# Even and odd weight rows, a subtraction moved to GpSimd, and three shifted steps in a mixture-of-experts kernel

## What is computed

```python
h = einsum('bsi,bio->bso', x, W[id]) + b[id][:, None, :]          # conditioning, 256 x 256 weights
xf = h.reshape(1024, 256)
y = (silu(xf @ sw1) * (xf @ sw3)) @ sw2                            # shared expert, 352 wide
scores = softmax(xf @ gate_w)                                      # 8 experts
weights, indices = top_k(scores, 2)
for e in range(8):                                                 # experts, 176 wide
    y += cw[:, e:e+1] * ((silu(xf @ rw1[e]) * (xf @ rw3[e])) @ rw2[e])
out = x + y
```

## Time and profile before

| | |
|---|---|
| median of three runs | 119.95 us |
| profiled execution, whole | 120.04 us |
| its span | 118.4 us |
| TensorE matmuls busy | 106.3 us, 90% of the span |
| DVE busy | 67.8 us, 57% |
| ACT busy | 52.2 us, 44% |
| Pool busy | 46.1 us, 39% |
| mean granted TensorE clock | 0.971 of full speed |
| bytes moved by DMA | 19.08 MB, mean 161 GB/s |

### The profile page before, as it was taken

How to read it: one execution, slowest core, us unless ns; L and a number is a source line. 1 busy time by engine, 2 the same in 40 slices (tenths; PEclk the granted TensorE clock), 3 DMA queues, 4 the chain that set the end, 5 groups by cost and what they waited for, 6 DMA issues and landing times.

```text
span 118.4 us, 2226 instructions
## 1 busy us (share of the span) xinstructions
PE 106.3 (90%) x624; PEld 90.0 (76%) x624; DVE 67.8 (57%) x221; ACT 52.2 (44%) x131; POOL 46.1 (39%) x62
## 2 busy tenths in 40 slices
PE   6887997706999999899999999999999999999791
PEld 4676886404678888667799989999999997888570
DVE  1044575037984199867878676577655543024951
ACT  4035575117161693255657755346555655103000
POOL 4360077730776200001653443443453635704400
PEclk9999999965699999999999999999999999999999
DMA  3899999998886257131223343241012110029843
GB/s 72 237 298 276 345 352 371 383 324 226 216 194 235 89 158 201 41 96 48 91 95 106 100 130 119 86 136 59 29 44 83 50 67 21 0 55 383 329 184 118
DMA packets 16737, 19.08 MB, mean 161 GB/s; under 512 B 2338, under 2 KB 13718, under 8 KB 16726
## 3 DMA queue, kind: packets, MB, share of 16 engines
q1 hardware_dynamic: 13302, 12.62, 35.5%
q0 software_dynamic: 1984, 4.46, 10.7%
q10 hardware_dynamic: 1440, 1.86, 4.7%
HBM read 12.64 MB, written 7.21 MB: 168 GB/s over the span
## 4 chain that ended last, share of the span: by engine, by line
PE 73%; DMA 8%; issue 6%; another core or an unknown queue 3%; POOL 3%; DVE 2%; ACTq 1%; ACT 1%; POOLq 1%; DVEq 0%
PE bank L846 52%; DMA y_area<-_out_by_choice_and_token 6%; PE bank L858 6%; PE bank L978 4%; PE bank L1013 4%; DMA _out_by_choice_and_token<-y_area,dest 2%; PE bank L876 2%; PE bank L873 1%; ACTq L306 1%; POOL _out_by_choice_and_token L406 1%; PE bank L875 1%; POOLq L287 1%; POOL cond_area L288 1%; POOL ids_bc L365 1%
## 5 line engine op out<-in xcount | busy, mean ns | idle before, releaser
L406 POOL DMA_INDIRECT _out_by_choice_and_token<-y_area,dest x23 | 23.6, 1025 | 40.7 <-DVE y_area L767 26.4
L394 POOL DMA_INDIRECT rows_by_expert<-h_area,slot x16 | 15.5, 971 | 15.9 <-DVE slot L628 11.6
L846 PE MATMUL bank<-w_all,hsT_hi 128*128 x72 | 21.6, 342 | 0.0
L846 PE MATMUL bank<-hT_area,sh_area 128*128 128x512 f32 (+1 forms) x72 | 18.7, 421 | 0.0
L846 PEld LDWEIGHTS bank<-hT_area,sh_area 128*128 128x128 f32 (+1 forms) x72 | 13.7, 193 | 4.2
L846 PEld LDWEIGHTS bank<-w_all,hsT_hi 128*128 128x128 f32 x72 | 13.0, 188 | 0.0
L761 DVE TENSOR_TENSOR y_area<-y_area,bank 128x176 f32<-128x176 f32 x23 | 7.7, 335 | 8.5 <-ACT y_area L503 4.3
L503 ACT ACTIVATE y_area<-bank 128x176 f32<-128x176 f32 x23 | 7.3, 318 | 10.1 <-PE bank L846 8.2
L846 PE MATMUL bank<-w_all,hsT_lo 128*128 x36 | 11.5, 320 | 0.0
L846 PE MATMUL bank<-raw,gT_f 88*128 x44 | 11.3, 378 | 0.0
L546 DVE TENSOR_TENSOR hsT_lo<-bank,hsT_hi 128x256 fp32r<-128x256 f32 x18 | 7.6, 423 | 6.3 <-ACT hsT_hi L499 5.5
(11 more groups left out here) (128 smaller groups left out, 198.2 us busy)
## 6 DMA issues: line engine op xcount, KB each, us to landing
h_area<-rows_by_expert SPq DMA_DIRECT2D x23, 128.0 KB
raw<-in_L_ffn_rw_dram SPq DMA_DIRECT2D x16, 176.0 KB
raw<-in_L_ffn_rw_dram SPq DMA_DIRECT2D x2, 704.0 KB
rows_by_expert<-x_area SPq DMA_DIRECT2D x8, 128.0 KB
y_area<-_out_by_choice_and_token SPq DMA_DIRECT2D x4, 256.0 KB, 4.4
y_area<-_out_by_choice_and_token ACTq DMA_DIRECT2D x4, 256.0 KB, 5.1
out_dram<-x_area SPq DMA_DIRECT2D x3, 256.0 KB, 2.1
sh_raw<-in_L_ffn_sw_dram SPq DMA_DIRECT2D x2, 352.0 KB, 5.0
```

Source lines behind the costliest of these rows:

```text
L394: nc.gpsimd.indirect_dma_start(out=rows_dram, out_offset=bass.IndirectOffsetOnAxis(ap=slot[:, i, t:t + 1], axis=0), in_=h_sb[:, t, :], in_ ...
L406: nc.gpsimd.indirect_dma_start(out=y_dram, out_offset=bass.IndirectOffsetOnAxis(ap=dest[:, j:j + 1], axis=0), in_=y_sb[j % NBY], in_offset ...
L846: last = nc.tensor.matmul(dst, w, v, start=start and n == 0, stop=stop and n == len(operands) - 1)
```

## The change

- *Even and odd rows.* Channels 2p and 2p + 1 now lie on partition p. This holds for the condition weights, the gate, sw1, sw3, rw1, rw3, and for rw2 with 88 partitions. Two rows of a weight are then one packet: 2,048 bytes for the condition weights and rw2, 2,816 for sw1 and sw3, 1,408 for rw1 and rw3. To match, `turn_x`, `condition`, the bias matmul and `turn_gated` read every second element of their stationary operand. `raw13` is laid out as (expert, w, k, F), so that rw1 and rw3 come in 8 loads in place of 16, and rw2 in 4 in place of 2. `w_all` keeps its layout; the casts into it read by a rearranged pattern.
- *The low part on Pool.* `sh_lo_of(0)` leaves DVE. Pool does the same subtraction after `dispatch(0)` and before the other three. The semaphore `sh_lo_ready` is split into one for Pool and one for DVE.
- *ranks(0)* stands ahead of the wait for `biasT` and of `turn_x(3)`.
- *shared_down.* Ahead of the loop only `shared_down(0, 0)` is left; `shared_down(0, 1)` goes behind the loop, to another bank. `acc_ready` now counts single products, and `base_of` is split in two.
- *The end.* The first token tile of sequence 3 is weighed on DVE in place of TensorE, its diagonals are not made, and `keep_warm` before the rows has 6 matmuls in place of 18.

```diff
 WARM_BEFORE_CONDITION = 3
-WARM_BEFORE_ROWS = 18
+WARM_BEFORE_ROWS = 6
...
-        raw13 = sb("raw13", [P, E, KD, 2, F])
-        raw13_rows = raw13[:, :, :, :, :].rearrange("p e k w f -> p e (k w f)")
...
+        raw13 = sb("raw13", [P, E, 2, KD, F])
...
-        y_acc = [bank[1], bank[4], bank[7], bank[6]]
+        y_acc = [[bank[1][:, 0:D], bank[5][:, D:2 * D]]] + [[bank[n][:, 0:D], bank[n][:, D:2 * D]] for n in (4, 7, 6)]
+        acc_ps = [None] + [bank[n][:, :] for n in (4, 7, 6)]
...
         sh_hi_ready = sem("sh_hi_ready")
-        sh_lo_ready = sem("sh_lo_ready")
+        sh_lo_pool = sem("sh_lo_pool")
+        sh_lo_dve = sem("sh_lo_dve")
...
         out_tiled = out.rearrange("b (p j) d -> b p (j d)", j=JS)
-        cond_w_tiled = cond_w.rearrange("e (k p) o -> e p k o", p=P)
+        cond_w_tiled = cond_w.rearrange("e (p k) o -> e p k o", k=KD)
...
+        def by_half(row):
+            return row.rearrange("p (k w f) -> p k w f", k=KD, w=2)
...
                 sp.dma_start(sh_raw[:, KD * w:KD * w + KD, :],
-                             src.rearrange("(k p) f -> p k f", p=P)).then_inc(sh_in, 16)
+                             src.rearrange("(p k) f -> p k f", k=KD)).then_inc(sh_in, 16)
...
                 for w, src in ((0, rw1), (1, rw3)):
-                    for k in range(KD):
-                        sp.dma_start(raw13[:, 2 * g:2 * g + 2, k, w, :],
-                                     src[2 * g:2 * g + 2, k * P:k * P + P, :]
-                                     .rearrange("e p f -> p e f")).then_inc(raw13_in, 16)
+                    sp.dma_start(raw13[:, 2 * g:2 * g + 2, w, :, :],
+                                 src[2 * g:2 * g + 2].rearrange("e (p k) f -> p e k f", k=KD)).then_inc(raw13_in, 16)
...
                 sp.dma_start(rows_dram[e * ROOM:e * ROOM + P, :], x_sb[:, 0, 0, :]).then_inc(filled, 16)
-            for c in range(2):
-                sp.dma_start(raw2[:, :, c, :],
-                             rw2[:, c * FH:(c + 1) * FH, :].rearrange("e p d -> p e d")).then_inc(raw2_in, 16)
+            for g in range(E // 2):
+                sp.dma_start(raw2[:, 2 * g:2 * g + 2, :, :],
+                             rw2[2 * g:2 * g + 2].rearrange("e (p c) d -> p e c d", c=2)).then_inc(raw2_in, 16)
...
-            for b in range(B):
+            dispatch(0)
+            pool.wait_ge(sh_hi_ready, 1)
+            nc.gpsimd.tensor_tensor(sh_lo[:, :, shared_cols(0)], sh_raw[:, :, shared_cols(0)],
+                                    sh_hi[:, :, shared_cols(0)].bitcast(F32), ALU.subtract).then_inc(sh_lo_pool, 1)
+            for b in range(1, B):
...
             act.dma_start(x_sb[:, 1], x_tiled[1]).then_inc(x_in[1], 16)
-            act.dma_start(gate_raw[:, :, :], gate_w.rearrange("(k p) e -> p k e", p=P)).then_inc(gate_in, 16)
+            act.dma_start(gate_raw[:, :, :], gate_w.rearrange("(p k) e -> p k e", k=KD)).then_inc(gate_in, 16)
...
                 if e == 0:
-                    act.wait_ge(raw13_in, 16 * 2 * KD * (E // 2))
-                nc.scalar.copy(w_all[:, e, HI13:LO13], raw13_rows[:, e, :]).then_inc(w13_hi_ready, 1)
+                    act.wait_ge(raw13_in, 16 * 2 * (E // 2))
+                nc.scalar.copy(by_half(w_all[:, e, HI13:LO13]), raw13[:, e].rearrange("p w k f -> p k w f")).then_inc(w13_hi_ready, 1)
...
                 if e == 0:
-                    act.wait_ge(raw2_in, 16 * 2)
+                    act.wait_ge(raw2_in, 16 * (E // 2))
...
             for b in range(BH, B):
-                act.wait_ge(acc_ready, b + 1)
-                nc.scalar.copy(acc_sb[b - BH][:, :], y_acc[b][:, :]).then_inc(acc_sb_ready, 1)
+                act.wait_ge(acc_ready, JS * (b + 1))
+                nc.scalar.copy(acc_sb[b - BH][:, :], acc_ps[b]).then_inc(acc_sb_ready, 1)
...
                 dve.wait_ge(sh_hi_ready, c + 1)
-                lo_part(sh_lo[:, :, cols], sh_raw[:, :, cols], sh_hi[:, :, cols]).then_inc(sh_lo_ready, 1)
+                lo_part(sh_lo[:, :, cols], sh_raw[:, :, cols], sh_hi[:, :, cols]).then_inc(sh_lo_dve, 1)
...
                 dve.wait_ge(w13_hi_ready, e + 1)
-                lo_part(w_all[:, e, LO13:ROW], raw13_rows[:, e, :], w_all[:, e, HI13:LO13]).then_inc(w13_lo_ready, 1)
...
-            def base_of(b):
-                dve.wait_ge(acc_ready, b + 1)
-                x_row = x_sb[:, b].rearrange("p j d -> p (j d)")
-                nc.vector.tensor_tensor(x_row, y_acc[b][:, :], x_row, ALU.add).then_inc(base_ready, 1)
+                lo_part(by_half(w_all[:, e, LO13:ROW]), raw13[:, e].rearrange("p w k f -> p k w f"),
+                        by_half(w_all[:, e, HI13:LO13])).then_inc(w13_lo_ready, 1)
...
+            def base_of(b, j):
+                dve.wait_ge(acc_ready, JS * b + j + 1)
+                nc.vector.tensor_tensor(x_sb[:, b, j, :], y_acc[b][j], x_sb[:, b, j, :], ALU.add).then_inc(base_ready, 1)
...
             hT_lo_of(3, 1)
-            sh_lo_of(0)
...
             dve.wait_ge(filled, 16 * E)
-            base_of(0)
+            base_of(0, 0)
...
                     w2_lo_of(s - 2)
-                if E + 4 <= s < E + 4 + NT // 2:
+                if E + 4 <= s < E + 4 + NT // 2 and s - E - 4 + NT // 2 != JS * (B - 1):
...
-            base_of(1)
+            base_of(0, 1)
+            dve.wait_ge(acc_ready, JS * BH)
+            x_row = x_sb[:, 1].rearrange("p j d -> p (j d)")
+            nc.vector.tensor_tensor(x_row, acc_ps[1], x_row, ALU.add).then_inc(base_ready, 1)
...
                 if i == 1:
-                    dve.wait_ge(combining, t + 1)
+                    dve.wait_ge(combining, min(t, JS * BH) + 1)
...
                 if b == 0:
-                    dve.wait_ge(base_ready, BH)
+                    dve.wait_ge(base_ready, JS + 1)
...
                 for j in range(JS):
-                    dve.wait_ge(weighed_ready, JS * (b - BH) + j + 1)
+                    if b == B - 1 and j == 0:
+                        dve.wait_ge(y_in[b], 16 * TOPK)
+                        for i in range(TOPK):
+                            weigh(b, i, j)
+                        continue
+                    dve.wait_ge(weighed_ready, min(JS * (b - BH) + j + 1, JS + 1))
...
                         last = nc.tensor.transpose(xT_ps[b][:, k * S + j * P:k * S + (j + 1) * P],
-                                                   x_sb[:, b, j, k * P:(k + 1) * P], ident[:, :])
+                                                   x_sb[:, b, j, :].rearrange("p (q k) -> p k q", k=KD)[:, k, :], ident[:, :])
...
                 for k in range(KD):
-                    last = nc.tensor.matmul(h_ps[b][m], cw_raw[:, b, k, m * P:(m + 1) * P],
+                    last = nc.tensor.matmul(h_ps[b][m], cw_raw[:, b, k, :].rearrange("p (q m) -> p m q", m=KD)[:, m, :],
...
                 if w == 0:
-                    pe.wait_ge(sh_lo_ready, c + 1)
+                    if c == 0:
+                        pe.wait_ge(sh_lo_pool, 1)
+                    else:
+                        pe.wait_ge(sh_lo_dve, c)
...
                 toks = slice(b * S + j * P, b * S + (j + 1) * P)
-                last = add_products(y_acc[b][:, j * D:(j + 1) * D],
+                last = add_products(y_acc[b][j],
...
                                      for c in range(NSH)], True, True)
-                if j == JS - 1:
-                    last.then_inc(acc_ready, 1)
+                last.then_inc(acc_ready, 1)
...
             for m in range(KD):
-                last = nc.tensor.matmul(bias_ps[:, m * B:(m + 1) * B], bias_rows[:, m * P:(m + 1) * P], one_hot[:, :],
+                last = nc.tensor.matmul(bias_ps[:, m * B:(m + 1) * B], bias_rows.rearrange("n (q m) -> n m q", m=KD)[:, m, :], one_hot[:, :],
...
             condition(1, 1)
+            ranks(0)
...
             turn_x(3)
-            ranks(0)
...
                 if j == 0:
-                    pe.wait_ge(raw13_in, 16 * 2 * KD * (E // 2))
+                    pe.wait_ge(raw13_in, 16 * 2 * (E // 2))
...
                 products = [(hsT[j % 2][:, k * P:(k + 1) * P],
-                             raw13[:, bass.ds(e, 1), k, :, :].rearrange("p e w f -> p (e w f)")) for k in range(KD)]
-                add_products(up_ps[j % 2], products, True, True).then_inc(up_ready, 1)
+                             raw13[:, bass.ds(e, 1), :, k, :].rearrange("p e w f -> p (e w) f")) for k in range(KD)]
+                add_products(up_ps[j % 2].rearrange("p (w f) -> p w f", w=2), products, True, True).then_inc(up_ready, 1)
...
                 for c in range(2):
-                    last = nc.tensor.transpose(gT_ps[j % 2][:, c * P:(c + 1) * P], gt[j % 2][:, c * FH:(c + 1) * FH],
+                    last = nc.tensor.transpose(gT_ps[j % 2][:, c * P:(c + 1) * P], gt[j % 2].rearrange("p (q c) -> p c q", c=2)[:, c, :],
...
                 if j == 0:
-                    pe.wait_ge(raw2_in, 16 * 2)
+                    pe.wait_ge(raw2_in, 16 * (E // 2))
...
             table()
-            for j in range(JS):
```

(7 more changed lines are left out.)

## The result

The changed kernel takes 115.55 us (median of 4 executions, 115.34 to 116.31), against 119.74 us for the kernel before on the same chip: a ratio of 0.964, 95% interval 0.959 to 0.969. Medians and ranges are of all executions of a kernel, ratios only of those within 1.5% of its fastest. The profiled execution took 115.34 us, with a span of 113.6 against 118.4.

The account below looks back on a forecast made before the run. TensorE's chain was taken as the bound, with a hole before ranks(2) from signals late during Pool's indirect stores. 120.04 - 6.47 + 2.2 - 1.35 - 0.87 = 113.55, less 0.09: 113.5 us, range 111.2 to 116.5.

Parts of the forecast that it names:

- the gap ahead of the fifth store: Sign on Pool: 1.6 us between its fourth and fifth indirect store, made by the subtraction placed there.
- the reductions: Sign on DVE: its reductions for tiles 4 to 7 come within 1 us from about 20.8 us.
- the second stretch: Late TensorE signals in the shared stage, during Pool's stores from 29.53 to 39.35 us; cost TensorE nothing before the change.
- What bounds the kernel: TensorE's chain, with 4.83 us idle before ranks(2) as signals come late during Pool's store rows, plus 1.64 of low clock.
- The pause: Pool's subtraction between stores four and five lets tiles 4 to 7 through in time: -6.47 us, bounds 0 to -6.47.
- What comes back: Twelve stores in a row make gate 2 late in the shared stage: +2.2 us, bounds 0 to 5.0.
- One shared_down less at first: One of two products goes from ahead of the loop to behind it: net -1.35 us.
- Tile (3, 0) on DVE: At the end, after the last read of y, TensorE does one product, DVE two weighings: -0.87 us, bounds 0 to -1.0.
- Packets, strided operands: Longer weight-load packets are hidden, and loads of every second element as stationary operand cost nothing: 0 each.
- Rival (c): Strided loads cost twice 122 ns, mainly in turns of gated tiles: slower, 121.1 us; chance 0.11.
- Rival (a): Late signals stay, as full DMA engines at 1.13 share cause them, not the stores: 117.7 us; chance 0.22.
- Rival (b): Row of twelve stores takes back the pause's gain through shared-stage holes and low clock: about 119.5 us; chance 0.12.

Follow-up runs that it names:

- b_loads_late: Kernel before, with SP's queue issuing the second half of raw13, fills, raw2 and shared down weights only after the eighth logits; ratio 1.037.
- b_stores_late: Kernel before, with Pool waiting for the eighth logits before its first indirect store, so all sixteen run in one row; ratio 1.019.
- b_pause: Kernel before, with only Pool's subtraction of the shared expert's low part added between its fourth and fifth indirect store; ratio 0.972.
- a_lo_dve: Changed kernel, with the low part of the shared expert's first columns back on DVE, so no pause in Pool's stores; ratio 0.988.
- after: The changed kernel itself, in its profiled execution of 115.34 us; median 115.55 us, ratio 0.964 to the kernel before.
- a_30_pe: Changed kernel, with tile (3, 0) weighed by TensorE's diagonal products again; ratio 0.959 to the kernel before.
- a_pool_late: Changed kernel, with Pool waiting for the eighth logits before its fifth store, for a longer pause; ratio 0.972.
- v_open: Changed kernel, with Pool's subtraction between its second and third store and DVE's second low part before its wait for the ranks; 113.83 us, ratio 0.950.
- a_down_first: Changed kernel, with shared_down(0, 1) back ahead of the loop, still 6 warming matmuls at the end; ratio 0.962.
- after_again: The changed kernel run once more, unaltered; 116.00 us, ratio 0.960, seven executions between 114.46 and 120.32 us.
- b_down_late: Kernel before, with only shared_down(0, 1) moved behind the loop and 6 warming matmuls in place of 18; ratio 0.989.
- b_layout: Kernel before, with only the even and odd rows, their loads and strided operands; ratio 1.004.

## Why the prediction was right, and by how much

Forecast 113.5 us, measured 115.55, inside its range. The kernel got faster for the forecast's reason, but by 4.2 us and not by the 6.5 of its sum. Of the signs that it gave, the gap ahead of the fifth store came (1.19 us for 1.6), and a loop that starts well ahead of 48.4 us. The others failed: TensorE was idle for 1.83 us, the clock was at 0.50 from 22.1 to 25.5 us, the reductions ran from 21.32 to 23.39, the first turn of rows came at 43.94 (up to 43.5 was forecast), and the last addition ended 3.0 us after the last read of y (1.65 was forecast). The upper end of the range had been set for 5.0 us coming back in the second stretch and little gained at the end. Little was gained at the end, but the second stretch took 0.6 us, and the rest was lost in the first. So it is in part luck that the time lies within the range. By its steps:

- *What bounds the kernel*: right, and shown by b_loads_late and b_stores_late. The reading of the two late stretches was the step on which all hung.
- *The pause*: right in kind, too large in size, and this is the step that failed. The forecast took -6.47 and +2.2, together -4.3 us; the runs have -3.4 (b_pause) and -2.9 (a_lo_dve). The interval of b_pause alone reaches from 2.4 to 4.4 us, so it is the traces that tell what was missed. The forecast said that the signals of tiles 4 to 7 would be the first late thing, and that they would be in time once stores four and five stood apart. But the signal of the last condition, one step ahead of them, can be late in stores one to four. ACT read it 1.6 us after its matmul in four traces, at 20.38 to 20.41 us whatever the fifth store did (after, a_30_pe, a_lo_dve, a_pool_late), and 0.5 us after in the kernel before, whose first store stands 0.16 us later. With the pause behind the second store it read it after 0.03 us (v_open). In the profiled executions of b_pause, a_down_first and after_again it came within 0.6 us, and then the ranks were late in stores five to eight. Either way a stall that ends between 21 and 30 us is left, and in the changed kernel's profiled execution half of the low clock with it. One gap doesn't end the trouble of the first row, it cuts it in two.
- *What comes back*: priced at 2.2 us for a row of twelve stores. In the changed kernel's profiled execution no such row formed, as `ranks(2)` ran only at 25.53 and made a second gap of 2.3 us; the second stretch took 0.6 us. In the execution of after_again it formed, and took 1.15 and 4.4.
- *One shared_down less at first*: -1.35, measured -1.35 (b_down_late, within 0.4 to 2.4; a_down_first does not confirm it).
- *Tile (3, 0) on DVE*: -0.87, measured 0 (a_30_pe). The forecast's bound of 0 was "DVE late from its first eight", and that is the case: they end at 109.40 us, behind the last read at 108.34. The end did get 0.8 us shorter, counted from the last scatter (10.76 us after it, 11.57 before), but for another reason: the reads of y took 7.8 us and not 9.1. In the nine traces with 6 warming matmuls they took 7.7 to 8.9 us, in the five with 18 of them 9.0 to 9.1. What shortens them was not settled; b_down_late shows only that the late product and the fewer warming matmuls are enough for part of it.
- *Packets, strided operands*: 0, measured 0.4% slower together (b_layout), by an interval that just excludes none. Rival (c) did not come: the load is longer by 38 ns and not by 122, and hidden in a loop 0.1 us longer, where (c) put 5.6 us.

The terms as measured, -3.1, -1.35, 0 and +0.4, make 115.9 us from 119.95; the median was 115.55. As each of the first two is known only within about 1 us, the match is no proof that nothing is missing.

Rival (a) is refuted. Rival (b) is real, but seen in one profiled execution, the slowest of seven. That it is also what makes the other executions of the changed kernel differ by some us is likely and not shown: the traces differ in which of the signals slips, and that decides how the stores fall into rows.

## What to carry to other kernels

When a consumer waits for a signal that by the trace was long due, and the profile names no engine for it, look at what Pool is doing: here a row of indirect stores stood beside each such wait. Try Pool's other work between the stores ahead of the moment a signal is due and not behind it, and keep work that doesn't need the signal in front of the wait; the kernel that does both had the lowest median here, 113.83 us (v_open). And when two engines share the end of a kernel, add up each one's work from the moment it can start: taking work from the one that waits and giving it to the one that is full brings nothing.

## What the runs showed of the hardware

- TensorE's signals come late while Pool runs indirect stores one after another, 1.27 us apart. With a DMA share of 0.18 to 0.37 (b_loads_late) the last one is as late as with 1.1, and with 1.10 and no stores none is (b_stores_late). With 1.19 us between the fourth store and the fifth, the logits that were 3 to 5 us late came in time, but signals could be late again in the four stores behind it: DVE read the ranks 3.4 us late in b_pause. In rows of twelve and sixteen stores an engine stood 7.26 and 7.37 us waiting for one. By what path a row of stores holds them was not tried.
- The order in which the stall falls is not stable. The same kernel showed it ahead of the logits in one execution and behind the ranks in another, whose first store started 0.11 us later (14.62 and 14.73 us).
- DVE's weighing and Pool's addition disturb each other. One row for each operation of the changed kernel's `x_area` (count, then minimum, median and maximum ns):
```profile
L817 DVE SCALAR_TENSOR_TENSOR x_area<-y_area,weight,x_area x10: 469/472/1490, 104.1 to 110.5; 128x256 f32<-128x256 f32 x10
L425 POOL TENSOR_TENSOR x_area<-acc_sb,x_area x2: 1510/1511/1512, 104.2 to 106.8; 128x512 f32<-128x512 f32 x2
```
  Two of the ten weighings, the ones that meet Pool's additions, take about 1.49 us in place of 0.47. Pool's two take 1.51 us here. Where they start as a weighing ends, as in the earlier trace rows, they take 1.26, and the weighing that they meet is as slow (1.52 us there). The Trainium skill, page "SBUF — State Buffer", section "SBUF: two separate sides", says that a DVE operation with two SBUF inputs and a GpSimd operation that reads SBUF exclude each other for the whole instruction. The trace agrees: 1.49 is the weighing's own 0.47 and 1.0 of the addition.
- A stationary operand that takes every second fp32 element loads in 160 ns and not 122 (88 columns). By the Trainium skill's rule that the prediction cites ("SBUF — State Buffer", section "Door 1: The DMA port swizzle") it would have been free; the measurement decides, though behind the loop's matmuls it cost 0.1 us at most.
